# Decoder layer with a sparse expert stage: gate and residual applied per expert tile, a last stage that adds two halves

## The chip, the cores and the metric

One core of one Trainium2 chip runs the whole program. The metric is the device time of one execution in microseconds; lower is better. Times are medians of several runs, and one execution is profiled instruction by instruction.

## What is computed

The program runs a decoder layer on 32 sequences of 128 rows of 128 numbers: a recurrent attention block, a cross attention, and a sparse feed-forward block with eight experts. Only the last of the three is touched here. Each row goes to its two best experts, and the results come back weighted by the two gates, plus the row itself:

```python
logits = jnp.einsum('bsh,eh->bse', x, Wr)
probs = jax.nn.softmax(logits, axis=-1)
top_v, top_i = jax.lax.top_k(probs, K)                  # K = 2
top_v = top_v / jnp.sum(top_v, axis=-1, keepdims=True)
...
for e in range(E):
    w_e = jnp.sum(jnp.where(top_i == e, top_v, 0.0), axis=-1)
    h = jnp.einsum('bsh,mh->bsm', x, W1[e]) + b1[e]
    h = jax.nn.gelu(h, approximate=False)
    y = jnp.einsum('bsm,hm->bsh', h, W2[e]) + b2[e]
    out = out + y * w_e[..., None]
...
x = _layernorm(x + _L0_ffn_ref(x, ...), axis=-1)
```

## The kernel before

Five engines run hand-written programs that meet only at semaphores. The program has four stretches: a setup; a loop over eight groups of four sequences (attention, cross attention, routing); the expert stage; and the last stage.

**Routing.** In the group loop VectorE (DVE) computes for each row its two experts, its place in each expert's region of the DRAM tensor `expert_in`, and two gates, which it keeps in `gate_all` (lines 1283 to 1288). GpSimd (POOL) writes each row twice into `expert_in` by indirect DMA, once for each expert. A row there is 132 words: 128 of data, one that says where the result goes (`home`), and three unused. POOL also copies the normalised rows `xb` into `x_all` (line 845), as the residual for later.

**Expert stage.** 72 tiles `j` of 128 rows, all rows of a tile for one expert. Tile `j` passes through these steps:

- SP loads 128 rows of data into `xt` (four buffers, line 485) when the buffer's former rows have been transposed (`turned`), and the four further words into `home` (eight buffers, line 491) when an earlier result has been written out (`y_out`).
- TensorE (PE) transposes the rows (`turn_rows`, line 1767), two tiles ahead; DVE copies them out (`turned_rows`, line 1353) and copies the expert's first weights and bias into `w1c` (`weights`, line 1359), whose address it reads from the table `tab` with a register load (`value_load`, shown as TENSOR_LOAD).
- PE multiplies with the first weights (`hidden`, line 1774, one tile ahead), ScalarE (ACT) applies four Gelus (line 670), and PE multiplies with the second weights (`outputs`, line 1783). The order on PE is transpose `j + 2`, hidden `j + 1`, outputs `j`.
- DVE adds the bias and moves the result to `ysb`, which is the tile `xa` (`results`, line 1367). POOL writes it to DRAM `expert_out` at its `home` by indirect DMA (line 858).

PE and DVE run this in loops of four tiles, POOL and SP of eight, ACT of 24. On DVE the order is copy `j + 2`, weights `j + 2`, results `j`.

**Last stage.** `expert_out` holds for each row its two results side by side. SP waits for all results, then loads groups of four sequences (512 KB, four buffers `two_rows` in the tile `mix`, line 516). For each of eight groups: ACT multiplies the first result by its gate (`first_part`, line 686), POOL adds the residual from `x_all` (`first_sum`, line 872), DVE multiplies the second result by its gate and adds (line 1399), takes the statistics (lines 1405 and 1409), POOL forms scale and shift in four small steps (`last_scale`, lines 878 to 888), ACT normalises (`last_norm`, line 695), and SP stores the 256 KB (line 522). A buffer is loaded again when its group has been combined.

```python
                for t in range(T):
                    nc.vector.scalar_tensor_tensor(
                        out=acc[m][:, t, :], in0=two_rows[m][:, t, 1, :],
                        scalar=gate_all[:, bass.ds(g * T + t, 1), 1],
                        in1=acc[m][:, t, :], op0=ALU.mult, op1=ALU.add).then_inc(combined, 1)
```

## Time and profile before

| | us |
|---|---|
| median of 3 runs | 866.14 |
| the 3 runs | 862.64, 866.14, 867.37 |
| the profiled execution | 862.9 |
| its span, first to last instruction | 861.0 |
| setup and group loop, up to the first transpose of an expert tile | 658.6 |
| from the first outputs to the last (71 tile steps and one product) | 149.0 |
| from there to the end, the last stage mostly | 47.7 |

A row of the timeline gives the start in us, the duration, the engine, the line, the operation with its tiles, and in brackets how long the engine was idle before and what it waited for. `x8` is the number of instructions merged into the row; a 128x128 float32 product shows as two instructions, so `x8` is four products. Names are those of the underlying tiles without numbers: `xnT` is the transposed rows, `qT` the first weights and bias, `hT` the hidden values, `w_t` the second weights, `xa` the results, `xn` the loaded rows, and `x`, `x1b`, `xbk`, `cumg` the sums of the last stage. `PEld` is TensorE's weight load, and a `q` behind an engine's name is its instruction queue.

### The profile page before, as it was taken

What the parts mean: (1) busy time and instruction counts of PE and PEld (TensorE: products, weight loads), DVE (VectorE), ACT (ScalarE), POOL (GpSimd) and SP (SyncE); (2) the same over time, 40 slices, a digit from 0 to 9 for tenths busy, and PEclk for the clock granted to TensorE, in tenths of its full rate; (3) what the DMA queues carried; (4) which work ended last, traced back from release to release, by engine and by line L of the source; (5) the groups of instructions that cost most, each with busy time, mean ns of one, the idle gap of its engine ahead of it and who ended that gap; (6) DMA issues with size and microseconds to landing.
All of it is one profiled execution on the core that took longest, in us unless ns stands there. A gap on an engine that the chain in (4) does not pass through costs nothing.

```text
span 861.0 us, 21597 instructions
## 1 busy us (share of the span) xinstructions
PE 667.3 (78%) x6159; PEld 480.8 (56%) x6160; DVE 537.5 (62%) x1725; ACT 378.1 (44%) x798; POOL 367.9 (43%) x514
## 2 busy tenths in 40 slices
PE   4325988978988888978988988988963999999700
PEld 1212645744744754754753763754653999989700
DVE  3585567678677677677677776676673444444343
ACT  2002164354454454454454444444521555555455
POOL 2524172254255155156056056057033555455555
PEclk9555998999999999999999999999895999999955
DMA  7500000000000000000000000001204222222153
GB/s 252 203 0 13 1 30 11 2 22 16 0 19 19 0 19 19 0 19 19 0 19 19 0 19 19 0 4 34 71 31 95 63 65 65 62 59 65 47 171 122
DMA packets 45528, 36.43 MB, mean 42 GB/s; under 512 B 20059, under 2 KB 39452, under 8 KB 45249
## 3 DMA queue, kind: packets, MB, share of 16 engines
q1 hardware_dynamic: 37312, 23.09, 9.6%
q0 software_dynamic: 4608, 9.59, 3.3%
q10 hardware_dynamic: 3584, 3.48, 1.2%
q8 instruction: 9, 0.15, 0.1%
q14 instruction: 15, 0.12, 0.0%
HBM read 23.35 MB, written 12.76 MB: 42 GB/s over the span
## 4 chain that ended last, share of the span: by engine, by line
PE 47%; DVE 19%; issue 12%; POOL 11%; ACT 4%; DMA 3%; DVEq 1%; POOLq 1%; SPq 0%; ACTq 0%
PE bank L1783 8%; PE bank L1774 8%; PE bank L1492 8%; PE bank L1529 5%; POOL rstd L769 4%; PE bank L1650 3%; POOL expert_in L798 3%; PE bank L1637 2%; DVE negmax L1179 2%; PE bank L1619 2%; PE bank L1577 2%; DVE stats L1063 2%; PE bank L1658 2%; DVE xn L1072 2%; PE bank L1585 1%
## 5 line engine op out<-in xcount | busy, mean ns | idle before, releaser
L766 POOL TENSOR_SCALAR vare<-mv 128x1 f32<-128x1 f32 (+1 forms) x112 | 25.6, 229 | 279.6 <-DVE mv L1068 277.6
L858 POOL DMA_INDIRECT expert_out<-xa,home x72 | 80.1, 1112 | 81.0 <-DVE xa L1367 44.4
L670 ACT ACTIVATE hT<-bank,qT 128x128 f32<-128x128 f32 x288 | 81.7, 369 | 63.1 <-PE bank L1774 61.9
L1783 PE MATMUL bank<-w_t,hT 128*128 x576 | 80.6, 283 | 3.9 <-ACT hT L670 3.9
L798 POOL DMA_INDIRECT expert_in<-xb_rows,slot_u x72 | 73.8, 1025 | 22.4 <-issue 17.4
L1179 DVE TENSOR_REDUCE negmax<-bank 128x4 f32<-128x512 f32 x128 | 79.4, 683 | 3.9 <-PE bank L1619 3.1
L565 ACT ACTIVATE mix<-bank 128x512 f32<-128x512 f32 x128 | 66.1, 603 | 33.6 <-PE bank L1637 32.0
L1774 PE MATMUL bank<-xnT,qT 128*128 128x128 f32 x576 | 79.8, 283 | 0.1
L1492 PE MATMUL bank<-xqT,w_qkv 128*128 128x512 f32 x144 | 73.0, 623 | 5.1 <-DVE x L1168 5.1
L1783 PEld LDWEIGHTS bank<-w_t,hT 128*128 128x128 f32 x576 | 69.9, 191 | 6.4 <-issue 4.9
L1774 PEld LDWEIGHTS bank<-xnT,qT 128*128 128x128 f32 x576 | 71.5, 195 | 3.2 <-issue 2.6
L769 POOL TENSOR_TENSOR rstd<-vare,minus_half 128x1 f32<-128x1 f32 (+1 forms) x112 | 67.6, 604 | 9.9 <-POOL vare L766 0.9
L1112 DVE TENSOR_TENSOR hT<-bank,decay 128x512 f32<-128x512 f32 x72 | 46.4, 686 | 28.1 <-PE bank L1529 28.0
L1359 DVE COPY qT<-w_t 128x516 f32 x72 | 31.0, 431 | 43.9 <-issue 39.6
L565 ACT ACTIVATE hebT<-bank 128x512 f32<-128x512 f32 x36 | 21.5, 597 | 64.5 <-PE bank L1577 64.5
L1367 DVE TENSOR_TENSOR xa<-bank,b_bc 128x128 f32<-128x128 f32 x72 | 21.0, 292 | 41.8 <-PE bank L1783 29.5
L1492 PE MATMUL bank<-w_qkv,xqT 128*128 128x512 f32 x72 | 42.0, 673 | 5.7 <-ACT mix L565 5.2
L1529 PE MATMUL bank<-qT,kT 64*128 64x128 f32 x576 | 41.8, 285 | 1.5 <-DVE hT L1112 1.4
L1492 PEld LDWEIGHTS bank<-xqT,w_qkv 128*128 128x128 f32 x144 | 25.7, 197 | 29.9 <-issue 22.2
L565 ACT ACTIVATE cT<-bank 128x512 f32<-128x512 f32 x32 | 19.1, 597 | 52.2 <-PE bank L1650 52.2
L1650 PE MATMUL bank<-mix,vpad 128*32 128x128 f32 x1024 | 36.7, 287 | 6.3 <-DVE hT L1112 5.4
L1492 PE MATMUL bank<-xnT,w_ff 128*128 128x512 f32 x64 | 37.5, 742 | 4.9 <-ACT xnT L565 4.9
(290 smaller groups left out, 1399.3 us busy)
## 6 DMA issues: line engine op xcount, KB each, us to landing
xn<-expert_in SPq DMA_DIRECT2D x72, 64.0 KB
mix<-expert_out SPq DMA_DIRECT2D x8, 512.0 KB, 4.0
ctxT<-in_ctxT SPq DMA_DIRECT2D x9, 256.0 KB
w_t<-in_w_t ACTq DMA_DIRECT2D x1, 2064.0 KB, 7.8
xT_all<-in_xT SPq DMA_DIRECT2D x4, 512.0 KB, 5.6
x_all<-in_x SPq DMA_DIRECT2D x4, 512.0 KB, 9.2
w_t<-in_w_t SPq DMA_DIRECT2D x1, 2048.0 KB, 7.8
expert_in<-xb_rows,slot_u POOLq DMA_INDIRECT x72
```

The lines of the kernel that those rows point to most:

```text
L565: nc.scalar.activation(dst, src_ap, func, scale=scale, **kw).then_inc(free[BANK[name]], 1)
L670: ins = nc.scalar.activation(hx[n][:, c, :], bank[2 + n][:, c * P:(c + 1) * P], ACT.Gelu, bias=w1c[n][:, FF + c:FF + c + 1])
L769: nc.gpsimd.tensor_tensor(rstd[stage][:, t:t + n], vare[stage][:, t:t + n], minus_half[:, 0:n], ALU.pow).then_inc(rstd_ready[stage], n)
L798: nc.gpsimd.indirect_dma_start(xs[:, :], bass.IndirectOffsetOnAxis(ap=slot_u[:, t, k:k + 1], axis=0), xb_rows[k][:, t, :], None).then_inc( ...
L858: nc.gpsimd.indirect_dma_start(ys[:, :], bass.IndirectOffsetOnAxis(ap=home[:, n, 0:1].bitcast(U32), axis=0), ysb[n % UNROLL], None).then_i ...
L1112: nc.vector.tensor_tensor(at[t % 2][:, r, :, :], b[:, :].rearrange("p (a n) -> p a n", a=PAIRS), decay[:, t, :].unsqueeze(1).broadcast_to( ...
L1179: nc.vector.tensor_reduce(negmax[t % 2][:, i, 28:28 + XC], b[:, :].rearrange("p (c n) -> p c n", c=XC), AX.X, ALU.max, negate=True).then_i ...
L1492: done(mm(b[:, :], lhsT, rhs, start=True, stop=True), name)
L1529: ins = mm(halves[r][:, tile(p)], kT[rows, p, tile(t)], qT[rows, p, tile(t)], start=True, stop=True)
L1650: ins = mm(b[32 * i:32 * i + 32, tile(c)], vpad[:, t, 4 * c + i, :], pT[t % 2][:, i, c, :], start=True, stop=True)
L1774: ins = mm(bank[2 + n % 2][:, c * P:(c + 1) * P], w1c[n % 2][:, c * P:(c + 1) * P], xtT[n % 2], start=True, stop=True)
L1783: ins = mm(bank[4 + n % 2][:, 0:P], hx[n % 2][:, c, :], w2_t[:, bass.ds(e, 1), c, :].rearrange("p a n -> p (a n)"), start=(c == 0), stop=( ...
```

## The change

- **Routing.** The two gates are written into word 129 of the rows that go to `expert_in` (`GATE`). Word 130 (`OWN`) is 1 in the first copy of a row and 0 in the second. POOL no longer copies `xb` into `x_all`. One small memset comes at the start.
- **Expert stage.** ACT gets one more step for each tile, `own_rows`: the loaded rows times `OWN`, into the tile `xab` (`own`), after the Gelus of that tile. DVE gets one more, `weighed`: result times gate plus own rows, in place. POOL's write now waits for that. SP loads the next rows into a buffer only when `own_rows` has read the old ones (`own_ready`). The Python loops of PE, DVE, ACT and POOL are written out for all 72 tiles; SP keeps its loop. DVE loads the expert number once for each tile and not twice. Some waits that others imply are gone.
- **Last stage.** `expert_out` is laid out by partition, so that a load of a group reads 4 KB in one piece for each partition, with 32 KB from one partition's piece to the next; before it read pieces of 1 KB. All eight loads are issued at once, the last four into `x_all`. DVE adds the two halves in one instruction for each group and takes the statistics. ACT's first step and POOL's sum are gone. Loops are written out here too.

```diff
@@ SP @@
             def row_in(j, n, row):
                 sp.wait_ge(turned, j + 1)
+                sp.wait_ge(own_ready, j + 1)
                 sp.sem_inc(sp_held, 1)
                 sp.dma_start(xt[n % UNROLL], xs[bass.ds(row, P), 0:P]).then_inc(x_in[n % UNROLL], 16)
...
-            both = ys[0:SEQS * P * TOPK, :].rearrange("(s p k) n -> p s (k n)", p=P, k=TOPK)
+            both = ys[0:SEQS * P * TOPK, :].rearrange("(p s k) n -> p s (k n)", p=P, k=TOPK)
+
+            for g in range(G):
+                sp.dma_start(two_rows[g].rearrange("p t k n -> p t (k n)"), both[:, g * T:g * T + T, :]
+                             ).then_inc(y_back[g], 16)
+            for g in range(G):
+                sp.wait_ge(outc_ready, g + 1)
                 sp.sem_inc(sp_held, 1)
...
+                sp.dma_start(A["out"][:, g * T:g * T + T, :], out_tiles[g % 2][:, :, :]).then_inc(stored[g % 2], 16)
@@ ACT @@
-            def first_part(g, m, turns):
...
+            def own_rows(j):
+                act.wait_ge(x_in[j % UNROLL], 16 * (j // UNROLL + 1))
+                act.wait_ge(home_in[j % (2 * UNROLL)], 16 * (j // (2 * UNROLL) + 1))
+                nc.scalar.activation(own[j % UNROLL], xt[j % UNROLL], ACT.Copy,
+                                     scale=home[:, j % (2 * UNROLL), OWN - P:OWN - P + 1]).then_inc(own_ready, 1)
+
+            act.sem_inc(own_ready, UNROLL)
+            for j in range(TILES):
+                gelu(j)
+                own_rows(j)
+
+            def last_norm(g):
                 act.wait_ge(rstdc_ready, g + 1)
...
+                if g >= 2:
+                    act.wait_ge(stored[g % 2], 16 * (g // 2))
@@ POOL @@
-                pool.wait_ge(xn_ready[LNB], ln_nth(g, T - 1) + 1)
-                pool.sem_inc(pool_held, 1)
-                nc.gpsimd.tensor_copy(x_all[:, bass.ds(g * T, T), :], xb[:, :, :]).then_inc(xkept, 1)
...
-            def first_sum(g, m):
@@ DVE @@
-                nc.vector.reciprocal(gate_all[:, bass.ds(g * T, T), 0], wsum[:, :])
+                nc.vector.reciprocal(xb_rows[0][:, :, GATE], wsum[:, :])
...
-            def results(j, i, n):
-                e = dve.value_load(tab[0:1, 0, bass.ds(j, 1)], min_val=0, max_val=EXP - 1)
...
+            def weighed(j):
+                n = j % (2 * UNROLL)
+                dve.wait_ge(own_ready, j + 1 + UNROLL)
+                dve.wait_ge(y_drained, j + 1 + 2)
+                nc.vector.scalar_tensor_tensor(
+                    out=ysb[j % UNROLL], in0=ysb[j % UNROLL], scalar=home[:, n, GATE - P:GATE - P + 1],
+                    in1=own[j % UNROLL], op0=ALU.mult, op1=ALU.add).then_inc(y_added, 1)
...
+            for j in range(TILES):
                 if j + 2 < TILES:
...
+                    turned_rows(j + 2)
+                    experts.append(expert_of(j + 2))
+                    weights(j + 2, experts[j + 2])
+                results(j, experts[j])
+                weighed(j)
...
+            def combine(g):
+                m = g % 4
+                dve.wait_ge(y_back[g], 16)
+                if g >= 4:
+                    dve.wait_ge(outc_ready, g - 3)
+                    dve.sem_inc(dve_held, 1)
+                nc.vector.tensor_tensor(acc[m][:, :, :], two_rows[g][:, :, 0, :], two_rows[g][:, :, 1, :], ALU.add
+                                        ).then_inc(combined, 1)
```

On DVE one tile of the expert stage stands like this before, inside the loop of four tiles. ISA rows set registers; `bank5` is the PSUM bank of the outputs, `qT` the first weights.

```order
L1352 REGISTER_ALU [waits turned]
L1353 COPY xnT<-bank1 128x128 [waits h_mm]
L1357 ISA
L1357 TENSOR_LOAD tab
L1357 ISA x2
L1359 ISA [waits gelu_done]
L1359 COPY qT<-w1_t 128x516
L1363 ISA
L1363 TENSOR_LOAD tab
L1363 ISA x2
L1367 ISA [waits y_out1,y_mm]
L1367 TENSOR_TENSOR xa<-bank5,b2_bc 128x128
```

After the change, from the results of one tile to those of the next:

```order
L1323 TENSOR_TENSOR xa<-bank4,b2_bc 128x128
L1331 SCALAR_TENSOR_TENSOR xa<-xa,home,xab 128x128 [waits y_drained,own_ready]
L1308 COPY xnT<-bank1 128x128 [waits h_mm,turned]
L1311 TENSOR_LOAD tab
L1311 ISA x2
L1316 ISA [waits gelu_done]
L1316 COPY qT<-w1_t 128x516
L1323 ISA [waits y_mm]
L1323 TENSOR_TENSOR xa<-bank5,b2_bc 128x128
```

One instruction is new between the results and the next copy, and it waits for the instruction right ahead of it; the second register load and the register steps on the loop's counter are gone.

On ACT two tiles of the expert stage stand like this before:

```order
L667 REGISTER_ALU
L670 ACTIVATE hT<-bank3,qT 128x128 [waits y_mm,h_mm]
L670 ACTIVATE hT<-bank3,qT 128x128 x3
L667 REGISTER_ALU
L670 ACTIVATE hT<-bank2,qT 128x128 [waits y_mm,h_mm]
L670 ACTIVATE hT<-bank2,qT 128x128 x3
```

And after, from the same place:

```order
L660 ACTIVATE hT<-bank3,qT 128x128 [waits y_mm,h_mm]
L660 ACTIVATE hT<-bank3,qT 128x128 x3
L667 ACTIVATE xab<-xn,home 128x128 [waits home_in3,x_in3]
L660 ACTIVATE hT<-bank2,qT 128x128 [waits y_mm,h_mm]
L660 ACTIVATE hT<-bank2,qT 128x128 x3
L667 ACTIVATE xab<-xn,home 128x128 [waits home_in4,x_in0]
```

A fifth activation stands behind each four. At the start of this stage the load of the activation table stood behind a wait for the first hidden product (`h_mm`), and now stands ahead of it.

On SP the last stage stands like this before, with its loads (line 516) and stores (line 522) in turn:

```order
L516 DMA mix<-expert_out 128x4x256 [waits y_out3,combined,y_out2,y_out0,y_out1]
L516 DMA mix<-expert_out 128x4x256 [waits combined] x3
L526 UNCONDITIONAL_BRANCH
L522 DMA out<-x2 128x512 [waits outc_ready]
L516 DMA mix<-expert_out 128x4x256 [waits combined]
L522 DMA out<-xb_rows0 128x4x128 [waits outc_ready]
L516 DMA mix<-expert_out 128x4x256 [waits combined]
```

And after:

```order
L516 DMA mix<-expert_out 128x1024 [waits y_out2,y_out3,y_out1,y_out0]
L516 DMA mix<-expert_out 128x1024 x3
L516 DMA x_all<-expert_out 128x1024 x4
L521 DMA out<-x2 128x512 [waits outc_ready]
L521 DMA out<-xb_rows0 128x4x128 [waits outc_ready]
L521 DMA out<-x2 128x512 [waits outc_ready]
```

All eight loads stand ahead of the first store in the one queue.

## Rows read from the trace of the kernel before

**Rows 1.** Two windows: us; busy us (count) of PE, PEld, DVE, ACT, POOL; clock

```profile
664.30:813.33 149.03, 145.97 (x1205) 140.14 (x1205) 65.89 (x210) 82.86 (x286) 78.52 (x71) 1.00 0.25 62
813.33:861.00 47.67, 0.00 (x0) 0.00 (x0) 19.56 (x97) 23.01 (x64) 25.48 (x42) 0.53 0.44 135
```

**Rows 2.** Timeline of PE in the last tiles, which are written out

```profile
806.06 1.06 PE L1774 MATMUL bank<-xnT,qT 128*128 128x128 f32 x8
...
807.96 1.06 PE L1774 MATMUL bank<-xnT,qT 128*128 128x128 f32 x8
808.85 1.06 PE L1783 MATMUL bank<-w_t,hT 128*128 x8
```

**Rows 3.** The table load on ACT, and POOL's copy in the last group

```profile
L670 ACT ACT_TABLE_LOAD  x3: 1283/1283/1283, 661.6 to 763.4; - x3
...
637.59 0.61 POOL L845 COPY x_all<-xb_rows 128x512 f32 x1
```

**Rows 4.** Timeline of DVE, in the loop and in the written-out last tiles

```profile
692.63 0.28 DVE L1353 COPY xnT<-bank 128x128 f32<-128x128 f32 x1
...
693.48 0.43 DVE L1359 COPY qT<-w_t 128x516 f32 x1 [0.56 <-issue]
...
808.36 0.28 DVE L1353 COPY xnT<-bank 128x128 f32<-128x128 f32 x1
809.02 0.43 DVE L1359 COPY qT<-w_t 128x516 f32 x1 [0.38 <-issue]
810.05 0.29 DVE L1367 TENSOR_TENSOR xa<-bank,b_bc 128x128 f32<-128x128 f32 x1 [0.60 <-PE bank L1783]
```

**Rows 5.** DVE steps that wait for the one before, and line 1399's duration

```profile
643.47 0.17 DVE L1319 TENSOR_SCALAR n_rows<-n_rows 128x8 f32<-128x8 f32 x1
643.67 0.17 DVE L1320 CAST n_rows_i<-n_rows 128x8 int32<-128x8 f32 x1
...
627.38 0.18 DVE L1068 BATCH_NORM_AGGREGATE mv<-stats 128x2 f32<-128x6 f32 x1 [0.15 <-DVE stats L1063]
...
L1399 DVE SCALAR_TENSOR_TENSOR x1b<-mix,gate_all,x1b x8: 347/348/354, 827.5 to 843.2; 128x128 f32<-128x128 f32 x8
```

**Rows 6.** ACT: four Gelus in the timeline, and one copy with a scale

```profile
809.05 1.14 ACT L670 ACTIVATE hT<-bank,qT 128x128 f32<-128x128 f32 x4 [0.76 <-PE bank L1774]
...
L686 ACT ACTIVATE xf<-mix,gate_all x16: 384/386/402, 821.1 to 844.1; 128x128 f32<-128x128 f32 x16
```

**Rows 7.** SP's first loads of rows, PE's wait for them, landing of line 491

```profile
656.73 2.14 SPq L485 DMA_DIRECT2D xn<-expert_in  x4
...
658.59 0.47 PE L1767 MATMUL bank<-ident,xn 128*128 128x128 f32 x1 [17.32 <-DMA xn<-expert_in]
...
DMA to landing us min/median/max: 0.8/1.6/1.9
```

**Rows 8.** Timeline of the last stage: first two loads in use

```profile
821.13 1.31 ACT L686 ACTIVATE xf<-mix,gate_all 128x128 f32<-128x128 f32 x4 [9.16 <-DMA mix<-expert_out]
822.63 1.28 ACT L686 ACTIVATE xab<-mix,gate_all 128x128 f32<-128x128 f32 x4 [0.19 <-DMA mix<-expert_out]
```

**Rows 9.** The page's costliest groups: an addition of 128x512 on DVE

```profile
L1112 DVE TENSOR_TENSOR hT<-bank,decay 128x512 f32<-128x512 f32 x72 | 46.4, 686 | 28.1 <-PE bank L1529 28.0
```

**Rows 10.** Timeline of the last stage: the last group

```profile
851.33 0.87 DVE L1405 BATCH_NORM_STATS2 stats<-cumg 128x6 f32<-128x128 f32 x4
...
852.74 0.23 POOL L878 TENSOR_SCALAR varec<-mvc 128x4 f32<-128x4 f32 x1 [0.49 <-DVE mvc L1409]
...
854.83 1.65 ACT L695 ACTIVATE xb_rows<-cumg,shiftc,rstdc 128x128 f32<-128x128 f32 x4 [0.90 <-POOL shiftc L888]
856.57 0.37 SPq L522 DMA_DIRECT2D out<-xb_rows  x1
```

**Rows 11.** Landing times of the stores (line 522), and a load at the start

```profile
DMA to landing us min/median/max: 2.0/2.4/2.6
...
x_all<-in_x SPq DMA_DIRECT2D x4, 512.0 KB, 9.2
```

229 lines of the change are left out of this document (74 added, 155 removed).

## The prediction

> **What bounds the kernel now.** I read the windows first. From the first outputs of the expert stage to the last, 149.0 us pass, and PE is busy in 146.0 of them; no other engine passes 83 us [rows 1]. Then PE is idle for 47.7 us while DVE, ACT and POOL are busy 20, 23 and 25 us: no engine bounds the last stage, the chain through all of them does [rows 1]. So I treat the two stretches apart.
>
> The expert stage takes 71 steps and one product: (149.03 - 1.06) / 71 = 2.08 us for each tile. The timeline of PE shows what a tile costs where nothing disturbs it: hidden to hidden 1.90 us (806.06 to 807.96), the outputs start 0.89 after the hidden product, and a product of eight takes 1.06 [rows 2]. These tiles are in written-out code. PE's floor is thus 1.90; the other 0.18 are loop turns, register work and the three table loads of ACT, one at each turn of its loop [rows 3].
>
> **Part 1, the expert stage.** PE's work stays the same. What can hold it is DVE. DVE's results of tile j wait for PE's outputs j; only behind them come the copy and the weights of tile j + 3, and PE needs these for hidden j + 3, which stands ahead of outputs j + 2. That circle closes over two tiles. Step by step, in written-out code:
>
> - End of outputs to start of results: 808.85 + 1.06 = 809.91 to 810.05, 0.14 [rows 2, 4].
> - Results 0.29 [rows 4], then the gap to an instruction that waits for the one before. In written-out code it is 0.03 (643.47 + 0.17 to 643.67); in the loops it is up to 0.15 [rows 5].
> - The new `weighed`: not in this trace, but the same form on the same shape is line 1399, 0.35 [rows 5].
> - Copy to weights, start to start, with one register load between: 0.66 written out, 0.85 in the loop [rows 4]. Weights 0.43 [rows 4].
> - Hand-over to PE: I allow 0.05, as DVE's gap for itself [rows 5] with some room.
> - Hidden j + 3 to the end of outputs j + 2: 0.89 + 1.06 = 1.95 [rows 2].
>
> The sum is 0.14 + 0.32 + 0.35 + 0.66 + 0.43 + 0.05 + 1.95 = 3.90 for two tiles, **1.95 for each**. Without `weighed` it would be below twice the floor, so today PE leads and afterwards DVE does, by a little. The lower end is PE's floor, 1.90. The upper end takes the loop's values (gap 0.15, copy to weights 0.85): 4.21 for two, 2.11 each. I take 1.95, since after the change all of this is written out. That gives 71 x 1.95 + 1.06 = 139.5 us, a gain of **9.5**; the ends are 136.0 (gain 13.0) and 150.9 (loss 1.9).
>
> ACT's new `own_rows` costs 0.39 [rows 6]. ACT is idle 0.76 us before each four Gelus [rows 6], so it is hidden; without that cover it would delay the outputs by what is left over. ACT's table load of 1.28 us [rows 3] now comes before PE's first product instead of after it. PE then still needs its first Gelus at a low clock, so I take a gain of **0.9**, between 0 and 1.3. The last tile's `weighed` lies open, with its gap: **-0.35**. Half the register loads of DVE go; the 0.66 above has that in it already.
>
> POOL's copy of `xb` in the group loop is dropped, 0.61 us at 637.59 [rows 3], eight times 4.9 us. Behind it stands the scale of the last row tile, and DVE asks for that only after its routing (line order in the code: `heb_norm(g + 1, 3)` behind `chosen`), so what is late next is DVE itself: I count nothing. Should it all lie open, the gain would be 4.9, which I hold excluded by that order. The gates are the same instructions with another target. SP's new wait is the third rival below.
>
> **Part 2, the last stage.** The first load is in use at 821.13, the second 1.5 us later [rows 8]; the loads need 1.5 each. I rebuild the stage on the clock of before:
>
> - Group 0: DVE adds 128x512. Nearest is line 1112, 0.69 [rows 9]; gap 0.03; from the first statistics to POOL's first small step 1.41 (851.33 to 852.74), from there to the norm 2.09 (to 854.83), the norm 1.65 [rows 10]. So the norm starts at 821.1 + 0.72 + 1.41 + 2.09 = 825.3 and its store is issued at 827.1.
> - Cadence: DVE needs about 0.72 + 1.3, POOL about 2.09, and the two output tiles a circle: norm 1.65, 0.09 to the store, landing 2.4 [rows 11], 0.1 to the next norm, 4.24 for two groups. All three lie between 2.0 and **2.12 for each group**.
> - Do the first stores land in time? Eight loads are ahead of them in one queue. They end at 821.1 + 7 x 1.5 = 831.6. A load at the start of the program, issued behind four others, took 9.2 us to land [rows 11]: later transfers of the queue wait for earlier ones. So store 0 lands at about 832.3, norms 2 and 3 start at 832.4 and 834.1, norms 4, 5, 6, 7 at 836.6, 838.3, 840.9, 842.5, and norm 7 ends at 844.15.
> - From the end of the last norm to the end of the span: 861.0 - 856.48 = 4.5 [rows 10]. The end is at 848.7, a gain of **12.3**. If the stores did not wait for the loads, norm 7 would start at 825.3 + 7 x 2.12 = 840.1 and the gain would be 14.7.
>
> I take the first, by the 9.2 us of that load. The Trainium skill (DMA: Bandwidth & Descriptors, section on HWDGE ordering) says that a transfer's semaphore increment is a strongly ordered write which lands only after every earlier write of that DMA engine; by it the gain is 12.3, without it 14.7.
>
> **The sum**, against the profiled execution's 862.9: 862.9 - 9.5 - 0.9 + 0.35 - 12.3 = 840.5. The median of the runs shown is 866.1, 3.2 above the profiled one, which is near the fastest of them. A later median may lie anywhere in that spread; I add half of it and say **842**.
>
> **Rivals.**
>
> *The expert stage gives nothing.* If the new instruction's gap and the register load cost what they cost in the loops, the DVE circle is 2.11 a tile, and the 9.5 turn into -1.9: 842 + 11.4 = 853.4. For it: those rows are the majority of the trace. Against: the written-out tiles show both smaller [rows 4, 5].
>
> *The loads slow down.* The pieces are now 32 KB apart for neighbouring partitions. If a load took 3.0 us and not 1.5 (half the rate of rows 8), the last would land at 842.1, and the end is 842.1 + 0.72 + 1.41 + 2.09 + 1.65 + 4.5 = 852.5, 3.8 later than in the sum: 846. Against: the load at the start also reads 4 KB pieces, 16 KB apart, and its 9.2 us are what four equal loads ahead of it at 1.5 each and a landing explain [rows 11]. 
>
> *Slower: the rows come too late.* SP now loads tile k + 4 only after `own_rows` k. From the start of hidden k: 1.06 for the product, 1.14 for four Gelus, 0.39 for the copy [rows 2, 6], with a hand-over 2.6; SP's turn at most 0.5 (four issues take 2.14 [rows 7]); landing L; the transpose 0.11; and PE goes on with hidden k + 3. So a tile takes at least (3.2 + L) / 3. In an empty machine L is 658.59 - 656.73 = 1.86, which gives 1.69, no bound. Line 491's small loads, made beside all other traffic, land in 1.9 at most [rows 7]. From L = 2.65 the wait bounds the stage, from 3.8 it eats all gains: at L = 3.9 a tile takes 2.37, the stage 169.3 (+20.3), and the time is 862.9 + 20.3 - 0.9 + 0.35 - 12.3 = 870.4, with the same 1.5 added 872.
>
> **How the numbers follow.** I give the forecast 0.62, the first rival 0.22, slow loads 0.08, late rows 0.08. The forecast's own bounds: all lower ends together (13.0, 1.3, 14.7) make 862.9 - 13.0 - 1.3 + 0.35 - 14.7 = 834.3; the upper side is the first rival's 853.4, with 1.5 for the spread of medians 855. The range 834 to 855 leaves out late rows and part of the tails, about 0.15. A measurement of this kernel can tell about 0.5%, or 4 us, from no change. Every case but late rows is faster by more; of that one's 0.08 I count 0.02 as no change and 0.06 as slower.
>
> **What would show it.** Right: `weighed` on DVE near 0.35 with its gap below 0.1; hidden to hidden near 1.95, with PE's waits before hidden released by DVE's weights; no wait of the transposes for `expert_in`; from the last outputs to the end near 36 us in place of 47.7; ACT's norm of group 2 waiting for the first store's landing, near the last load's. The first rival: hidden to hidden near 2.1. The second: DVE's additions waiting for loads more than 2.2 us apart. The third: PE's transposes waiting for `xn`, and SP's loads issued right after `own_rows`. I would be wrong about the mechanism if PE's idle time in the expert stage were released by ACT, or if written-out code itself made the sequencers late, which I have not priced beyond the ends above.

## The result, and the profile after

| us | before | after |
|---|---|---|
| median of the runs shown | 864.55 (862.64 to 867.37) | 854.00 (850.31 to 859.38) |
| the profiled execution | 862.9 | 854.7 |
| up to the first outputs | 664.30 | 663.65 |
| from the first outputs to the last | 149.03 | 154.10 |
| from there to the end | 47.67 | 35.05 |

The ratio is 0.987, 95% interval 0.9835 to 0.9906. The forecast was 842 us: the time lies in the range, but the change brought less than half of what I expected. The parts tell why. The last stage gained 12.6 us, as forecast; the start gained 0.65; the expert stage, which was to gain 9.5 us, lost 5.1.

Later sets of runs, each with both kernels on one chip, gave medians of before from 856.7 to 868.8 and ratios of 0.9896, 0.9842 and 0.9807. So I compare times only within a set. Ratios with their intervals are those on record, estimated over the runs of both kernels; they can differ by some tenths of a per cent from the quotient of the two medians.

The two windows that answer to [rows 1], with the same columns:

```profile
663.65:817.75 154.10, 144.21 (x1206) 136.89 (x1205) 89.69 (x281) 101.32 (x355) 67.90 (x70) 0.99 0.25 62
817.75:852.80 35.05, 0.01 (x1) 0.00 (x0) 15.39 (x74) 13.17 (x32) 17.35 (x34) 0.52 0.50 184
```

PE was idle for 3.1 us of the stage before and is idle for 9.9 now, although no engine has become busier than PE. Something that is no engine's work holds it. The list of waits within the stage names it (engine, line, what it waited for: us in total, times, the longest):

```profile
PEld bank L1722 <- DMA xn<-expert_in: 8.4, 15, 1.5
...
PE bank L1722 <- DMA xn<-expert_in: 4.9, 7, 1.3
PEld bank L1722 <- issue: 2.8, 5, 1.0
```

Line 1722 is the transpose. In the kernel before it waited for `expert_in` only ahead of the first tiles [rows 7], and the stage's list of waits has no such row. This is the sign that the prediction gave for its third rival. One such place in the timeline:

```profile
692.84 0.53 SPq L487 DMA_DIRECT2D xn<-expert_in  x1
693.17 0.14 PEld L1722 LDWEIGHTS bank<-ident,xn 128*128 128x128 f32 x1 [1.47 <-DMA xn<-expert_in]
693.17 0.33 PE L1722 MATMUL bank<-ident,xn 128*128 128x128 f32 x1 [1.27 <-DMA xn<-expert_in]
```

The tiles between such places look as forecast:

```profile
697.02 0.27 PE L1722 MATMUL bank<-ident,xn 128*128 128x128 f32 x1
697.18 1.16 PE L1727 MATMUL bank<-xnT,qT 128*128 128x128 f32 x8
...
699.07 0.27 PE L1722 MATMUL bank<-ident,xn 128*128 128x128 f32 x1
...
699.38 0.29 DVE L1323 TENSOR_TENSOR xa<-bank,b_bc 128x128 f32<-128x128 f32 x1 [0.36 <-issue]
...
699.78 0.35 DVE L1331 SCALAR_TENSOR_TENSOR xa<-xa,home,xab 128x128 f32<-128x128 f32 x1
...
700.64 0.43 DVE L1316 COPY qT<-w_t 128x516 f32 x1 [0.31 <-issue]
700.97 0.27 PE L1722 MATMUL bank<-ident,xn 128*128 128x128 f32 x1
701.12 1.16 PE L1727 MATMUL bank<-xnT,qT 128*128 128x128 f32 x8
```

From transpose to transpose 2.05 and 1.90 us by turns. The `weighed` takes 0.35 with a gap of 0.11 ahead (699.38 + 0.29 to 699.78), and hidden starts 0.05 after DVE's weights end (700.64 + 0.43 to 701.12). The circle over two tiles is there, with 3.95 us where I had 3.90.

**How late the rows are.** A row of a wait shows only a part of it. PE's transpose follows the last instruction of the outputs ahead of it after 0.11 us where nothing holds it, start to start. What lies above 0.11, over tiles 3 to 71, I call the lateness of the rows. It is 0.0 us in the kernel before and 10.8 in the changed one, where 20 of the 69 transposes are more than 0.12 us late.

**SP's side of it.** The timeline of SP beside that of PE gives two numbers for each tile: how long after the transpose that frees a buffer its next load is issued, and how long before the next use the issue ends (its lead). Tiles 8 to 71 of the profiled executions:

| kernel | set | load issued after its buffer's transpose: median, longest | lead: shortest, median | stage |
|---|---|---|---|---|
| before | first | 2.89, 4.44 | 4.60, 5.04 | 149.0 |
| after | first | 6.07, 7.78 | 1.17, 1.95 | 154.1 |

The 20 late transposes had leads of 1.27 to 3.20 us, 1.73 in the median. Before, the shortest lead was 4.6: nothing that SP did showed. After the change the median is 1.95 and delays show at PE. A lead of 3.20 that is still too short says that the issue of the load is not all of it: some loads also land late.

**The code's own transfers.** The list of DMA queues has two that carry instructions. In the stage before, and after:

```profile
q14 instruction: 4, 0.03, 0.1%
q8 instruction: 2, 0.03, 0.1%
```

```profile
q8 instruction: 12, 0.20, 0.6%
q14 instruction: 13, 0.11, 0.2%
```

The transfers of q8 are 16 KB in one packet and those of q14 8 KB. One of q8 takes 0.9 to 1.6 us. The kernel before has two of these in the stage (at 666.95 and 813.02). Every version of the changed kernel, with its loops written out, has 12, in the execution above one each 11 to 16 us; with SP written out too (e2 below) those of q14 are 18 in place of 13.

What goes with them is late landings. Five traces of versions of the changed kernel (e1, e2, e3 twice, and the changed kernel in set 3) have the landing of some of the stage's loads on record (whole rows in e3, the `home` words in the others). Where no code transfer ran between issue and landing, none took more than 1.96 us (95 loads, medians 1.65 to 1.83); where one of 16 KB did, they took up to 3.63 (42 loads, medians 2.3 to 3.1). In the changed kernel's execution above 15 of the 69 loads had one between their issue and their transpose, and on these lie 6.6 of the 10.8 us; among them are seven of the nine transposes that came over 0.5 us late. Transpose 16, the one shown at 693.17, is one: its load was issued at 690.77, and a 16 KB transfer ran from 691.91 to 692.99. No run changes these transfers alone.

### The profile page after: what moved, and what is told of

Its sections match the earlier page's. It is cut to its first block, busy times and chain, and to the rows that moved or that the text cites. A ratio compares the mean times of both kernels' runs of the same rounds, so it can differ in the third digit from the quotient of the medians.

```text
span 852.8 us, 20643 instructions
## 1 busy us (share of the span) xinstructions
PE 668.4 (78%) x6159; PEld 479.0 (56%) x6159; DVE 557.1 (65%) x1772; ACT 386.7 (45%) x836; POOL 344.0 (40%) x499
## 4 chain that ended last, share of the span: by engine, by line
PE 36%; DVE 21%; issue 15%; POOL 11%; SPq 8%; ACT 3%; DMA 3%; DVEq 1%; POOLq 0%; ACTq 0%; another core or an unknown queue 0%
PE bank L1448 8%; PE bank L1485 5%; POOL rstd L747 4%; PE bank L1606 4%; PE bank L1727 3%; POOL expert_in L776 3%; PE bank L1593 3%; SPq L473 3%; PE bank L1575 3%; DVE negmax L1136 2%; PE bank L1533 2%; DVE stats L1020 2%; SPq L493 2%; SPq L487 2%; PE bank L1737 2%
## 5 line engine op out<-in xcount | busy, mean ns | idle before, releaser
L833 POOL DMA_INDIRECT expert_out<-xa,home x72 | 69.8, 970 | 96.4 <-DVE xa L1331 73.6
L1737 PE MATMUL bank<-w_t,hT 128*128 x576 | 77.2, 278 | 2.1 <-ACT hT L660 1.6
L1541 PE MATMUL bank<-w_out,hebT 128*128 128x128 f32 x288 | 40.6, 285 | 0.4 <-DVE hT L1069 0.4
L1722 PE MATMUL bank<-ident,xn 128*128 128x128 f32 x72 | 21.4, 298 | 24.7 <-DMA xn<-expert_in 22.1
```

Source lines behind the costliest of these rows:

```text
L833: nc.gpsimd.indirect_dma_start(ys[:, :], bass.IndirectOffsetOnAxis(ap=home[:, j % (2 * UNROLL), 0:1].bitcast(U32), axis=0), ysb[j % UNROLL ...
L1737: ins = mm(bank[4 + j % 2][:, 0:P], hx[j % 2][:, c, :], w2_t[:, bass.ds(e, 1), c, :].rearrange("p a n -> p (a n)"), start=(c == 0), stop=( ...
```

## Experiments

Each was profiled and run four to seven times beside the kernel before. `stage` is from the first outputs to the last in the profiled execution, and "lead" is as above. The kernel before was profiled in the first set only; where a stage of it is named, it is that one's 149.0 us.

### Set 1: four ways to have the rows earlier

```diff
@@ e1: own rows from other data, so that SP need not wait for them @@
-                sp.wait_ge(own_ready, j + 1)
-                nc.scalar.activation(own[j % UNROLL], xt[j % UNROLL], ACT.Copy,
+                nc.scalar.activation(own[j % UNROLL], x_all[:, j % UNROLL, :], ACT.Copy,
@@ e2: SP written out @@
-            with sp.Fori(0, TILES // (2 * UNROLL) - 1) as i:
+            for j in range(2 * UNROLL, TILES):
@@ e3: one load of 132 words for each tile @@
-                sp.dma_start(xt[n % UNROLL], xs[bass.ds(row, P), 0:P]).then_inc(x_in[n % UNROLL], 16)
-                sp.dma_start(home[:, n, :], xs[bass.ds(row, P), P:RW]).then_inc(home_in[n], 16)
+                sp.dma_start(xr[:, n, :], xs[bass.ds(row, P), :]).then_inc(x_in[n], 16)
@@ e4: eight row buffers @@
-        xt = [xn[:, n, :] for n in range(UNROLL)]
+        xt = [x_all[:, n, :] for n in range(2 * UNROLL)]
```

> The kernel after, but own_rows reads a fixed tile (x_all) in place of the loaded rows, so SP no longer waits for own_ready before it loads the next rows; the residual in the output is thus wrong data, the work on ACT and DVE is the same. In the kernel after, 154.1 us pass from the first outputs to the end of the last (663.65 to 817.75), undisturbed tiles alternate between 1.90 and 2.05 us, and about ten of the 72 transposes come 0.4 to 1.9 us late. Theory (the new wait takes the lead away: the load of rows for tile k + 4 starts after own_rows k, less than two tiles before PE wants it, so every hiccup of SP reaches PE): the stage shrinks to 71 x 1.98 + 1.2, so 141 to 145 us, and the time by 9 to 12. Rival A (SP's own pace of about 1.93 us a tile for two loads is too slow whatever it waits for): the stage stays above 150. Rival B (the longer chain on DVE holds PE): no change, 152 to 156.

> The kernel after with SP's loop over tiles written out too; waits, loads and all other engines as they are. Theory (short lead, plus an SP that has no pace to spare): the loop's turns and some register steps go, SP gets faster by 0.1 us a tile or so and catches up after a hiccup; the stage shrinks in part, to 145 to 150 us. If only the time from own_rows to the landing counts: no change, 152 to 156. If SP's pace alone counts: 143 or less.

> The kernel after with one load of all 132 words of a row per tile in place of two loads (rows and home words), into eight buffers; the waits ahead of it are the same two as before it (turned and own_ready of tile k for tile k + 4), so the lead is not longer. SP's work for a tile falls from about 1.93 us to about 1.2. If the lateness comes from SP being busy with the home words when own_ready arrives: stage 141 to 145 us. If it comes from the wait and the landing time alone: 152 to 156.

> The kernel after with eight row buffers in place of four: the load for tile k + 8 waits for own_rows k. Two loads per tile and SP's loop as in the kernel after. Theory (lead): the stage shrinks to 141 to 146 us. Rival A (SP's pace alone): the first tiles gain, then SP falls behind again, 149 or more.

Measured, beside a before of 856.36 us:

| | time | ratio, 95% | stage | lead: shortest, median |
|---|---|---|---|---|
| e1, no wait | 839.76 | 0.9776 (0.9690 to 0.9862) | 144.5 | 2.38, 3.57 |
| e2, SP written out | 838.75 | 0.9784 (0.9704 to 0.9863) | 144.9 | 1.59, 2.66 |
| e3, one load | 839.23 | 0.9787 (0.9701 to 0.9872) | 144.2 | 2.22, 2.59 |
| e4, eight buffers | 840.59 | 0.9795 (0.9717 to 0.9874) | 145.1 | 1.50, 3.11 |

All four come out alike, and the last stage is 35.1 to 35.3 us in each. That e1 helps speaks for the wait. That e2 and e3 help as much, with the wait in place, does not fit the wait alone: they make only SP's own work shorter. SP's list of waits shows the same. In e2, whose SP is written out, SP stands at the new wait in 40 tiles (first line, 660 to 800 us), in the changed kernel in three (second line, 664 to 818 us); in the others its own work makes it late:

```profile
SPq L486 <- ACT xab L666: 14.4, 40, 0.9
```

```profile
SPq L486 <- ACT xab L667: 1.7, 3, 1.1
```

This set has no run of the changed kernel beside it, though, so that its stage there is not known; sets 3 and 4 have one.

### Set 2: the wait alone, and its absence

b1 puts SP's new wait into the kernel before, with the copy on ACT that it waits for.

```diff
@@ e8: own rows one tile earlier, in eight buffers @@
             for j in range(TILES):
+                if j + 1 < TILES:
+                    own_rows(j + 1)
                 gelu(j)
-                own_rows(j)
@@ b1: in the kernel before @@
             def row_in(j, n, row):
                 sp.wait_ge(turned, j + 1)
+                sp.wait_ge(own_ready, j + 1)
...
                     gelu(i * in_turn + n, n % 2)
+                    own_copy(n % UNROLL, i * 16 * 6 + 16 * (n // UNROLL + 1))
@@ e5: no own rows, no weighing, no wait @@
-                sp.wait_ge(own_ready, j + 1)
-                own_rows(j)
-                weighed(j)
```

> The changed kernel as it is, again, so that it stands beside the variants on one chip. Four variants, each of which takes something different from the way of the row loads, all had an expert stage of 144.2 to 145.1 us, against 154.1 us in the profiled execution of the changed kernel; the kernel before also ran some 8 us shorter in their set than in the first set, though. Late rows as the cause: the stage here is again 150 to 155 us, with 8 or more PE transposes that wait for a row's DMA, and the kernel is 6 to 10 us slower than those variants in the ratio to before (0.985 to 0.99). Rival, that set of runs had a faster chip and the four edits did nothing: the stage is 144 to 146 us and the ratio about 0.978.

> Nothing taken away: ACT makes its own rows of tile k+1 before the Gelu of tile k instead of the own rows of tile k after it (8 own-row buffers instead of 4), so that SP's wait for them ends about one tile (2 us) earlier, close to the transpose that it already waited for. If the lateness of that wait is what costs, the stage comes down to that of the variant without the wait, 144 to 146 us, and no more than three transposes wait over 0.3 us for a row. If the cost lies in SP's own work for two loads a tile (1.9 us of each tile by the trace), or in ACT's extra operation, it stays where the changed kernel's stage is in this set.

> The kernel before with the new wait alone: ACT copies each row tile after its Gelu as in the changed kernel (no gate), and SP waits for that copy before it loads the tile four later. Its output is that of the kernel before. If the wait alone costs, whatever else the change does, the stage goes from 149.0 us to 152 to 156 us and transposes wait for `DMA xn<-expert_in`, most of all near the turns of SP's loop; the kernel is 3 to 7 us slower than before. If the lost gain has to do with PE's faster pace (1.98 instead of 2.07 us per tile), before's slower pace leaves SP its time and the stage stays within 1.5 us of 149.

> The changed kernel without the own rows (ACT), without the weighing (DVE) and without SP's wait for them: what the written-out loops alone make of the expert stage. The output lacks gate and residual. The first theory (DVE's circle of transposed copy, weights, results and weighing sets 1.975 us per tile, and a weighing costs it 0.35 us every tile) gives a stage of about 71 x 1.90 + 1.2 + 3 = 139 us: 5 us below the variant without the wait (144.5). If PE's own work and rows late by other causes set what is left, the stage stays at 143 to 145 us although DVE has 0.35 us less in every tile.

Measured, beside a before of 867.95 us:

| | time | ratio, 95% | stage | lead: shortest, median |
|---|---|---|---|---|
| after, again | 859.24 | 0.9896 (0.9862 to 0.9930) | 155.5 | 1.16, 1.59 |
| e8, own rows early | 857.53 | 0.9896 (0.9842 to 0.9950) | 151.1 | 1.28, 2.45 |
| b1, before with the wait | 874.10 | 1.0062 (1.0036 to 1.0088) | 154.8 | 1.10, 1.77 |
| e5, no gate, no residual | 853.53 | 0.9863 (0.9796 to 0.9930) | 148.9 | 1.23, 2.07 |

b1 shows that the wait, with the copy on ACT that it needs, costs by itself: 5.4 us by the ratio (3.1 to 7.6), in a kernel without any of the rest. This was the size expected. Its rows are late by 3.7 us in the stage, which is 5.8 longer than the 149.0 of the first set; its stage has one 16 KB code transfer, at its start.

e5 refutes the picture that only the wait matters. SP waits for nothing new there, and the stage is 148.9 us and not 139. Its timeline shows how SP falls back. At the start it loads right behind the transpose:

```profile
667.86 0.27 PE L1719 MATMUL bank<-ident,xn 128*128 128x128 f32 x1
669.12 0.33 SPq L486 DMA_DIRECT2D xn<-expert_in  x1
```

That load comes 1.3 us behind the transpose. At tile 17 it is 5.0, at tile 43 it is 7.7, and PE waits for rows by then:

```profile
744.36 0.33 PE L1719 MATMUL bank<-ident,xn 128*128 128x128 f32 x1 [0.93 <-DMA xn<-expert_in]
744.38 0.33 SPq L486 DMA_DIRECT2D xn<-expert_in  x1
744.97 0.33 SPq L492 DMA_DIRECT2D home<-expert_in  x1
746.29 0.33 SPq L486 DMA_DIRECT2D xn<-expert_in  x1
```

None of SP's rows shows a wait; it takes 1.91 us for a tile (744.38 to 746.29), and PE's floor is 1.90, so that the distance stays. The same in e8: the load starts 1.9 us after its transpose and drifts to 7 and more, so that its earlier start is used up. Its stage of 151.1 us misses the 144 to 146 that was expected of a mere lateness of the wait; it is shorter than that of the run beside it, but the two kernels' times can't be told apart. I had missed that **SP has a pace of its own**. In the changed kernel's loop it takes 1.90 us a tile, and at three tiles of each turn of eight 2.31, 2.09 and 1.98: 5 x 1.90 + 2.31 + 2.09 + 1.98 = 15.88 us, 1.985 a tile. PE of the changed kernel asks for a row each 1.975 us, PE of the kernel before each 2.08. So SP could win back its delays before, and can't now.

### Set 3: SP made faster, beside the changed kernel

e7 joins e3's single load, eight buffers and e2's written-out SP; its loads wait only for the results of the tile eight before to be written. e9 is e7 without own rows and weighing, and its output lacks gate and residual.

```diff
@@ e7 @@
-            def row_in(j, n, row):
-                sp.wait_ge(turned, j + 1)
-                sp.wait_ge(own_ready, j + 1)
+            def row_in(j, n, row, pace):
+                if pace is not None:
+                    sp.wait_ge(y_out[n % UNROLL], pace)
                 sp.sem_inc(sp_held, 1)
+                sp.dma_start(xr[:, n, :], xs[bass.ds(row, P), :]).then_inc(x_in[n], 16)
...
+            for j in range(2 * UNROLL, TILES):
+                row_in(j, j % (2 * UNROLL), row_of(j), 16 * ((j - 2 * UNROLL) // UNROLL + 1))
```

> The changed kernel, a third time, as the measure for the three beside it on this chip. Theory now: SP's own pace is what its row loads come by. Undisturbed, SP takes 1.90 us for a tile and 0.4, 0.2 and 0.1 us more at three tiles of each loop turn of eight (15.88 us per turn, 1.985 a tile), and now and then 0.6 to 1.2 us more; PE wants a row each 1.975 us, so that no lead can be won back, and the new wait starts it with 2.5 us of lead instead of 5. Stage 151 to 156 us here too, ratio 0.985 to 0.99. If the first set of variants owed its 144 to 145 us to its chip, and this one is like it, this one may show 145 to 147.

> The variant with one load of 132 words per tile instead of two (loop and both waits kept), once more, this time beside the changed kernel. SP's work per tile falls by about 0.65 us (a load's issue and its waits), so it can run ahead of PE to its wait again. Theory of SP's pace: lead at PE stays near 2.6 us, three or fewer transposes wait over 0.3 us, stage 6 us or more below the changed kernel's of this set. Rival, the chip and not the edit made the difference: within 2 us of the changed kernel.

> One load per tile, eight row buffers (SP waits only for the results of the tile eight before to have been stored), SP written out: SP has both the time and the lead. No transpose waits for a row except at the hiccup that all runs have near tile 49. What is left is the circle of the first theory (copy, weights, results, weighing: 1.90 and 2.05 us by turns, 1.975 mean): stage 71 x 1.975 + 1.2 + 2 to 3 = 143 to 144.5 us, and the kernel 1 us or more below the one with one load alone, if that one still lost some at single waits; the same if it did not.

> The same without own rows and without weighing (the output lacks gate and residual): neither SP nor DVE should bind any more, so that PE's own work is left. First theory's floor of 1.90 us a tile: 71 x 1.90 + 1.2 + 2 to 3 = 138 to 139 us, 5 us below the variant with the weighing. If the weighing costs DVE's circle nothing here (PE or Gelu set the pace in both), the two are within 1.5 us. An earlier run without gate and residual, with SP's two loads in a loop, showed 148.9 us: by the theory of SP's pace its gain was eaten by SP.

Measured, beside a before of 856.70 us:

| | time | ratio, 95% | stage | lead: shortest, median |
|---|---|---|---|---|
| after, third time | 843.23 | 0.9842 (0.9763 to 0.9922) | 147.6 | 1.53, 2.28 |
| e3 again, one load | 836.38 | 0.9758 (0.9682 to 0.9833) | 143.9 | 2.21, 2.60 |
| e7 | 836.53 | 0.9765 (0.9689 to 0.9840) | 143.2 | 3.16, 4.98 |
| e9 | 830.38 | 0.9674 (0.9601 to 0.9747) | 136.4 | not read |

The changed kernel's stage is shorter on this chip (147.6), which was the lesser of the two cases expected. The edit still helps: one load and not two takes 6.9 us off the median, and all four runs of it are faster than all four of the changed kernel; the profiled stage is 3.7 us shorter. e7's transposes wait for no row at all, and yet it is no faster than e3: from there on rows are no longer the bound.

The changed kernel's SP in this set shows both parts of the cause, its pace and what delays it:

```profile
672.84 0.33 SPq L487 DMA_DIRECT2D xn<-expert_in  x1
673.42 0.33 SPq L493 DMA_DIRECT2D home<-expert_in  x1
674.75 0.33 SPq L487 DMA_DIRECT2D xn<-expert_in  x1
675.41 1.19 SPq L493 DMA_DIRECT2D home<-expert_in  x1
677.66 0.33 SPq L487 DMA_DIRECT2D xn<-expert_in  x1
```

1.91 us from load to load (672.84 to 674.75), and then 2.91, since one issue takes 1.19 us in place of 0.33. A 16 KB code transfer runs on the DMA engines in that moment (675.28 to 676.23). This holds throughout: in the stages of all 18 traces 32 issues of SP take 0.8 us or more, and each of them overlaps a 16 KB code transfer, though such transfers fill at most 11% of a stage. How they hold up the issue isn't shown.

Intervals of 2.5 us and over between two loads number 4 in this execution, 5 in that of set 4 (below), 9 in the first one of the changed kernel and 13 in that of set 2, and the stages are 147.6, 150.3, 154.1 and 155.5. That the two rise together proves little: SP's loads follow PE's transposes, so their intervals add up to about the stage, whatever holds it. The lateness of the rows is the better measure: 5.8 us (4.4 of it on loads with a 16 KB code transfer), 6.5 (3.5), 10.8 (6.6) and 13.6 (5.0), in the same order. The kernel before has 4 such intervals too, and its transposes never wait. The longest issue of the second line of loads in this execution (duration in ns, min/median/max):

```profile
L493 SPq DMA_DIRECT2D home<-expert_in x72: 332/333/1663, 653.3 to 798.3; - x72
```

e9 gives PE's floor: 71 x 1.90 + 1.06 = 136.0 is the prediction's lower end, 136.4 is measured, below the 138 to 139 that was expected of e9.

```profile
658.82:795.20 136.38, 135.84 (x1206) 134.99 (x1205) 64.28 (x210) 80.95 (x284) 71.27 (x71) 1.00 0.25 68
```

In this window PE is idle for 0.5 us in all. Between e9 and e7 lie 6.8 us of stage: own rows on ACT and the weighing on DVE, together. DVE's circle accounts for 71 x 0.05 = 3.6 by my 1.95 and for 71 x 0.075 = 5.3 by the measured 1.975; that it is the whole isn't shown, since the run takes both steps away. Both runs have the 12 code transfers too, and with leads of 2.7 us and over their rows are never late.

### Set 4: SP made slower, and the weighing moved

```diff
@@ e10: e7 with the weighing on POOL, ahead of its write @@
+                nc.gpsimd.tensor_scalar(ysb[j % UNROLL], ysb[j % UNROLL], home[:, n, GATE - P:GATE - P + 1], None, ALU.mult
+                                        ).then_inc(y_scaled, 1)
+                pool.wait_ge(y_scaled, j + 1)
+                nc.gpsimd.tensor_tensor(ysb[j % UNROLL], ysb[j % UNROLL], own[j % (2 * UNROLL)], ALU.add
+                                        ).then_inc(y_added, 1)
@@ e11: the kernel before with a third load for each tile @@
                     home_of(n, row, i * 32 + (16 + 16 * (n // UNROLL)))
+                    again_of(j, row)
```

> The changed kernel once more, as the measure for those beside it. It had stages of 154.1, 155.5 and 147.6 us so far, the last on a chip where the kernel before is 1.3% shorter too. Theory of SP's pace: on any chip the x loads are issued 5 to 7 us after the transpose that frees their buffer, lead at PE about 2.3 us or less, and the stage is 147 to 156 us, longer the more single steps of SP take 0.6 us or more above its 1.9.

> The variant with one load per tile, eight row buffers and SP written out, again. Stage 143 to 144.5 us on a chip like the last, at most 147 on a slower one; 6 to 9 us below the changed kernel in time.

> That variant with the weighing moved from DVE to POOL, in two instructions (times gate, plus own rows) ahead of POOL's write of the results; nothing left out. The run without the weighing had a stage of 136.4 us against 143.2. If DVE's circle is what the weighing lengthens, the stage goes to 137 to 139 us, and the kernel 4 to 6 us below the one beside it. POOL then has about 1.0 us for its write and an estimate of 0.5 to 0.8 for the two instructions in a tile of 1.9 us, which just fits; if it does not, or if POOL's work slows DVE's, the stage is 143 us or more.

> The kernel before, with one more small load per tile on SP: 16 bytes of each row again, into a place that nothing reads; nobody waits for it in the stage. A measure of SP's pace by itself: its two loads and register steps take 1.9 to 1.99 us a tile, and a third with its steps adds an estimated 0.5 to 0.9. If SP's pace can bound the stage in spite of the five us of lead that the kernel before has, the tiles go from 2.07 to 2.4 to 2.9 us and the stage from 149 to 170 to 205 us, with transposes waiting for `DMA xn<-expert_in`. If only the new wait's latency mattered, the stage stays at 149 to 151.

Measured, beside a before of 868.78 us:

| | time | ratio, 95% | stage |
|---|---|---|---|
| after, fourth time | 853.11 | 0.9807 (0.9755 to 0.9859) | 150.3 |
| e7 again | 847.00 | 0.9760 (0.9698 to 0.9822) | 146.7 |
| e10, weighing on POOL | 925.05 | 1.0628 (1.0584 to 1.0672) | 213.3 |
| e11, before with a third load | 900.75 | 1.0346 (1.0308 to 1.0383) | 179.2 |

e11 settles the question of SP's pace. Nobody waits for the third load within the stage, no wait was added, and the kernel before has five us of lead, and still the stage is 30 us longer than the 149.0 of the first set. The loads' median issue moves from 2.89 to 8.4 us behind the transpose, 48 transposes are more than 0.12 us late, and a tile takes what SP takes:

```profile
801.13 0.33 SPq L487 DMA_DIRECT2D xn<-expert_in  x1
801.72 0.33 SPq L493 DMA_DIRECT2D home<-expert_in  x1
802.25 0.35 SPq L496 DMA_DIRECT2D again<-expert_in  x1
...
803.58 0.33 SPq L487 DMA_DIRECT2D xn<-expert_in  x1
```

2.45 us (801.13 to 803.58), with the turns of the loop 2.55 on the mean; 71 x 2.55 is 181 us, and 179.2 is measured. The third load, with the register steps that it needs, costs SP 0.55 us, though its issue shows 0.33 to 0.35.

e10 missed by far. POOL needs 3.06 us a tile (740.22 to 743.28):

```profile
740.22 1.04 POOL L830 DMA_INDIRECT expert_out<-xa,x_all  x1 [0.82 <-DVE xa L1320]
...
741.30 0.62 POOL L820 TENSOR_SCALAR xa<-xa,x_all 128x128 f32<-128x128 f32 x1
...
742.01 0.45 POOL L823 TENSOR_TENSOR xa<-xa,xab 128x128 f32<-128x128 f32 x1
...
743.28 1.04 POOL L830 DMA_INDIRECT expert_out<-xa,x_all  x1 [0.82 <-DVE xa L1320]
```

The bracket names DVE's results, which are long done; the write waits for the addition. The two instructions take 1.07, above my 0.5 to 0.8, and the write 1.04; what I left out is the idle time between the addition and the write, 0.82 us (742.46 to 743.28), and 0.13 at the other two joints. The weighing does not fit on POOL in this form, and whether taking it off DVE alone would give back e9's 6.8 us is not shown by it.

e7 repeats its gain over the changed kernel, 6.1 us by the medians here and 6.7 in set 3; in set 3 its four runs are all below the changed kernel's, here one of them (855.0) lies among these. It is the fastest complete version together with e3, which set 3 can't tell from it.

## Why the prediction was right and wrong

**The start: right in sign and size.** Forecast 0.9, measured 0.65. But PE's first outputs now take 1.92 us in place of 1.15:

```profile
663.65 1.92 PE L1737 MATMUL bank<-w_t,hT 128*128 x8
...
666.40 1.06 PE L1737 MATMUL bank<-w_t,hT 128*128 x8
```

The granted clock tells why (windows with the columns of [rows 1]; the first of after, the second of before). It was 0.52 under the first outputs, the lower level, and 1.00 under those of before:

```profile
663.70:665.50 1.80, 1.80 (x10) 1.80 (x10) 0.00 (x0) 1.43 (x5) 0.00 (x0) 0.52 0.18 37
```

```profile
664.30:665.50 1.20, 1.20 (x10) 1.20 (x11) 0.33 (x1) 0.80 (x4) 0.00 (x0) 1.00 0.30 56
```

PE had been at the low clock in both, after 17 us of idle time. In the records it rises at 663.1 us before and at 665.4 after, though PE's first transpose stands at 658.59 and 658.26. So the later rise matters more than the 0.65 us by which the outputs came earlier; why it came later isn't shown. The first step takes 2.75 us from outputs to outputs, 0.8 above the others, and I had not put that into the stage.

**The last stage: right.** Forecast a gain of 12.3, measured 12.6 (47.67 to 35.05), and 34.0 to 35.3 us long in all variants of the changed kernel but e10. Its rows, against [rows 10]:

```profile
825.52 0.69 DVE L1357 TENSOR_TENSOR x<-mix 128x512 f32<-128x512 f32 x1 [6.88 <-DMA mix<-expert_out]
826.37 0.87 DVE L1362 BATCH_NORM_STATS2 stats<-x 128x6 f32<-128x128 f32 x4 [0.16 <-DVE x L1357]
...
827.77 0.47 POOL L844 TENSOR_SCALAR varec<-mvc 128x4 f32<-128x4 f32 x1 [7.35 <-DVE mvc L1366]
...
829.45 0.68 POOL L850 TENSOR_TENSOR shiftc<-mvc,rstdc 128x4 f32<-128x4 f32 x1
...
830.60 1.65 ACT L680 ACTIVATE x<-x,shiftc,rstdc 128x128 f32<-128x128 f32 x4 [13.96 <-POOL shiftc L854]
...
832.36 0.34 SPq L521 DMA_DIRECT2D out<-x  x1
...
835.16 1.65 ACT L680 ACTIVATE x<-xbk,shiftc,rstdc 128x128 f32<-128x128 f32 x4 [0.76 <-DMA out<-x]
...
844.51 1.65 ACT L680 ACTIVATE x<-xbk,shiftc,rstdc 128x128 f32<-128x128 f32 x4 [0.49 <-POOL shiftc L854]
...
846.64 1.65 ACT L680 ACTIVATE xb_rows<-cumg,shiftc,rstdc 128x128 f32<-128x128 f32 x4 [0.49 <-POOL shiftc L854]
```

The addition takes the 0.69 of [rows 9]. The norms at the end are 2.13 us apart and wait for POOL, as the cadence of 2.12 said. With the stage's clock moved by 4.42 us (813.33 to 817.75), norm 7 was forecast for 842.5 + 4.4 = 846.9 and started at 846.64. But two errors cancel here. The first norm came 0.9 us later than worked out (5.08 after the first addition, forecast 4.2): POOL's first step took 0.47 and its third 0.68 where the last group shows 0.23 and 0.20. And the stores did not wait for the loads as long as I had put: ACT's third norm waited 0.76 us for the first store, which was issued at 832.36 and was thus landed at 835.1, 2.75 us after, near the 2.4 of a lone store [rows 11]. Landing times of the eight loads and of the eight stores:

```profile
DMA to landing us min/median/max: 3.7/6.6/9.2
...
DMA to landing us min/median/max: 2.0/2.3/2.8
```

The last load was issued at 825.2. The 3.7 is the first load's and the 9.2 the last one's in this trace, so that they landed from 825.5 to 834.4, one each (834.4 - 825.5) / 7 = 1.27 us, where I had put 1.5. My 831.6, on this clock 836.0, was 1.6 us late, and so the first store had little left to wait for. It landed 0.7 us after the last load. Whether it waited for it can't be read from this: the second store, with no load ahead of it, took 2.8 us. So the rule cited in the prediction is neither borne out nor refuted.

**The expert stage: wrong, by three terms.** Forecast 139.5, measured 154.1, 14.6 us apart.

- *Late rows, the larger part: the third rival's sum.* I had the right wait and the right sign of failure, and gave it 0.08. The failed step is "SP's turn at most 0.5". From the end of `own_rows` to the issue of the load that it frees pass 0.22 us at the least, but 1.08 in the median and up to 2.96, since SP's own cycle for one tile is 1.90 to 2.31 us, 1.985 on the mean: two loads, a register load and register steps, where I had taken only the four bare issues of 2.14 us [rows 7]. The formula tile >= (3.2 + L) / 3 asked whether the wait bounds a smooth stage. It does not, and where nothing disturbs SP the lead is 2.3 to 2.6 us against some 1.5 for a landing. What was missing is the second question: how fast does the issuing engine win back a delay? Before, it had 5 us of lead and PE's 2.08 a tile against its own 1.985; after, 2.6 us of lead or less and 1.975 against 1.985. b1, e11 and e3 show the two halves: the wait alone costs 5.4 us (3.1 to 7.6), a slower SP alone costs 32 us with no wait added, and a faster SP gives back 6.9 us with the wait in place. (The third rival's own sum has a slip too: by its formula and its -0.9, +0.35 and -12.3 the gains are gone from L = 3.6 on, not 3.8.)
- *The landing L had no tail in the sum.* I took 1.86 us and "1.9 at most" from a kernel with loops. With the loops written out, loads land up to 3.63 us after their issue while a 16 KB code transfer runs, and 6.6 of the 10.8 us of lateness lie on such loads. The prediction named late sequencers through written-out code as something it hadn't priced; what the traces show is near it, late landings and long issues. How the lateness divides between the lost lead and these transfers isn't shown: b1 is late by 3.7 us with hardly a transfer, e7 and e9 are not late at all with all 12 of them. It takes both the short lead and a delay.
- *The circle was mis-sized.* Without late rows (e7) the stage is 143.2 us, 2.00 for each step and not 1.95. The undisturbed tiles take 1.975, since the gap ahead of `weighed` is 0.11 and not 0.03; that is 71 x 0.025 = 1.8 us. The first outputs at the low clock are 0.8. The remaining 1.1 us are single tiles of 2.3 us that I have not followed. By the experiments' measure, e9 against e7, own rows and weighing together cost 6.8 us above PE's floor, and I had counted 3.6.

So 143.2 - 139.5 = 3.7 us are the circle and what stands beside it. The other 154.1 - 143.2 = 10.9 compare executions on two chips, but the lateness of the rows within the first one is 10.8. In set 3, on one chip, the two stages differ by 147.6 - 143.2 = 4.4 us, with 5.8 of lateness.

**The sum.** 862.9 - 0.65 + 5.07 - 12.62 = 854.7, the profiled execution. The first rival's time, 853.4, is close to it, but its cause isn't the one at work: `weighed` and the register load do not cost what they cost in the loops, as the rows above show.

**What stays open.** By what way a 16 KB code transfer lengthens SP's issue and a load's landing, and how much of the 14.6 us loops in place of the written-out code would save, wasn't tried. Long intervals of SP (2.5 us and over) are in b1 too (11), whose engines keep their loops and whose longest issue past the stage's start is 0.69 us, so code transfers aren't the cause of these. Why the same kernel's rows are late by 5.8 us in one execution and by 13.6 in another isn't known.

## What to carry to other kernels

A queue's engine has a pace, and it is to be counted like that of any other: all loads, register steps and loop turns of one tile, not the bare issues. When a wait is added to it, ask for the lead it leaves in tiles' time, and whether the engine is faster than its consumer, since only the difference wins a delay back. When loops are written out, look for the transfers of the code itself among the DMA queues, and at what lands late beside them. And a mean over all tiles of the kernel before isn't to be set against an undisturbed tile of the kernel after: each has its start and its single slow tiles.

## What I had not expected of the hardware

- One more load, with its register steps, costs SP 0.55 us (2.45 against 1.90 a tile, e11), while its issue shows 0.33. Single issues take up to 1.66 (set 3; 1.80 in e11), and all 32 of 0.8 us and over, in 18 traces, overlap a 16 KB code transfer.
- The loads of e3 and the `home` words land within 1.96 us of their issue where no code transfer runs, and take up to 3.63 where one of 16 KB does.
- Many executions, of the kernel before too, have one large gap near tile 49 (3.64 us from transpose to transpose before, 3.96 after, 5.67 in e7's second execution), in which SP's loads come late too. Others have none (e3, e9). Its cause wasn't tried.
- The same program's stage differed by 8 us between executions (147.6 to 155.5) with a granted clock of 0.99 to 1.00 in it; what goes with it is the lateness of the rows (5.8 to 13.6 us).
- Between an addition on POOL and POOL's indirect write that waits for it lie 0.82 us (e10), between two of its ordinary instructions 0.09.
